# Causal grouped attention: the division by the row sums moved onto VectorE, straight from the PSUM bank

## The reference

```python
def _attention(x, Wq, bq, Wk, bk, Wv, bv, Wo, bo):   # x is layer-normed, (b, t, n) = (2, 512, 256)
    b, t, n = x.shape
    hd = n // Q_HEAD                                  # 16 query heads of 16, 4 key and value heads
    q, k, v = x @ Wq.T + bq, x @ Wk.T + bk, x @ Wv.T + bv
    ...                                               # split into heads; _rope on q and k
    k = jnp.repeat(k, rep, axis=1); v = jnp.repeat(v, rep, axis=1)
    att = jnp.einsum('bhqd,bhkd->bhqk', q, k) / scale
    att = jnp.where(causal[None, None], att, -jnp.inf)
    att = jax.nn.softmax(att, axis=-1)                # exponentials divided by their row sums
    y = jnp.einsum('bhqt,bhtd->bhqd', att, v)
    y = y.transpose(0, 2, 1, 3).reshape(b, t, n)
    return y @ Wo.T + bo
x = x + _L1_attn_a_ref(_layernorm(x), ...)
```

## Time and profile before

| | |
|---|---|
| median of 3 runs | 1567.59 us (1562.62 to 1567.86) |
| the profiled execution | 1567.11 us, of which the span is 1565.3 us |
| TensorE busy, whole span | 1439.8 us (92%), 10620 matmuls |
| VectorE busy | 965.8 us (62%) |
| ScalarE busy | 756.6 us (48%) |
| in the stage, 1126 to 1140 us: TensorE, VectorE, ScalarE busy | 12.68, 9.67, 7.50 of 14.00 us |
| granted clock there | 1.00 |

### The profile page before, as it was taken

How to read it: one execution, slowest core, us unless ns; L and a number is a source line. 1 busy time by engine, 2 the same in 40 slices (tenths; PEclk the granted TensorE clock), 3 DMA queues, 4 the chain that set the end, 5 groups by cost and what they waited for, 6 DMA issues and landing times. The chain is left out here.

```text
span 1565.3 us, 29243 instructions
## 1 busy us (share of the span) xinstructions
PE 1439.8 (92%) x10620; PEld 1117.4 (71%) x10646; DVE 965.8 (62%) x2214; ACT 756.6 (48%) x1877; POOL 561.7 (36%) x556
## 2 busy tenths in 40 slices
PE   6999999999899899899999999998898898988897
PEld 4778777787689767677777766895565596733586
DVE  5666667666575665656565557548655754565663
ACT  5565656656235334343443443452545362598352
POOL 2835629354136254515333101552000173100173
PEclk9999999999999999999999999999999999998998
DMA  4122231222272343303021007335000534121534
GB/s 147 55 90 68 84 101 46 86 63 90 82 313 85 122 130 112 120 6 114 24 74 69 1 1 287 142 120 192 1 1 2 197 102 147 31 60 33 187 99 138
DMA packets 57453, 149.48 MB, mean 95 GB/s; under 512 B 10224, under 2 KB 24688, under 8 KB 57200
## 3 DMA queue, kind: packets, MB, share of 16 engines
q1 hardware_dynamic: 39664, 89.58, 16.7%
q0 software_dynamic: 17664, 58.21, 11.0%
HBM read 104.77 MB, written 38.27 MB: 91 GB/s over the span
## 5 line engine op out<-in xcount | busy, mean ns | idle before, releaser
L145 POOL TENSOR_SCALAR ln_var<-ln_moments 128x4 f32<-128x4 f32 x16 | 4.1, 253 | 403.7 <-DVE ln_moments L130 251.3
L412 POOL DMA_INDIRECT expert_rows<-s_y,s_to_row x92 | 90.9, 989 | 57.9 <-ACT s_y L736 36.9
L1370 ACT ACTIVATE s_scratch<-s_bank,s_neg_max 128x128 f32<-128x128 f32 (+3 forms) x128 | 67.2, 527 | 88.0 <-DVE s_neg_max L1460 87.9
L1460 DVE TENSOR_REDUCE s_neg_max<-s_bank 128x1 f32<-128x128 f32 (+3 forms) x128 | 59.4, 486 | 55.2 <-PE s_bank L1260 55.0
L2797 POOL TENSOR_TENSOR s_w_hi<-s_w_raw,zero 128x1024 fp32r<-128x1024 f32 x25 | 55.6, 2223 | 100.1 <-PE s_memory L81 77.1
L1258 PE MATMUL s_bank<-s_k,s_q 128*128 128x128 f32 (+3 forms) x256 | 88.6, 442 | 1.5 <-DVE s_v L1455 0.8
L2464 ACT ACTIVATE s_exps<-s_bank,s_rms 128x512 f32<-128x512 f32 x128 | 77.9, 690 | 13.5 <-PE s_bank L2363 11.0
L953 DVE TENSOR_TENSOR s_h_e<-s_bank,s_silu_e 128x176 f32<-128x176 f32 x92 | 31.4, 341 | 83.5 <-ACT s_silu_e L724 79.6
L79 PE MATMUL s_bank<-xn_t_hi,s_w_hi 128*128 128x512 f32 x192 | 79.6, 415 | 1.7 <-DVE xn_t_lo L212 1.2
L405 POOL DMA_INDIRECT s_xg<-normed_rows,s_from_row x64 | 63.6, 994 | 38.5 <-DVE s_from_row L848 20.2
L1277 PE MATMUL s_bank<-s_probs_t,s_v 128*128 128x512 f32 (+3 forms) x256 | 74.7, 435 | 2.5 <-ACT s_probs_t L1378 2.5
(11 more groups left out here) (428 smaller groups left out, 4856.4 us busy)
## 6 DMA issues: line engine op xcount, KB each, us to landing
s_expert_w_lo<-experts_lo SPq DMA_DIRECT2D x32, 608.0 KB, 12.9
s_e_lo<-in_experts POOLq DMA_DIRECT2D x32, 304.0 KB, 3.1
experts_hi<-s_e_hi POOLq DMA_DIRECT2D x32, 304.0 KB, 2.5
experts_lo<-s_e_lo POOLq DMA_DIRECT2D x32, 304.0 KB, 2.9
s_expert_w_hi<-experts_hi SPq DMA_DIRECT2D x16, 608.0 KB, 12.1
s_w_raw<-in_wa_o SPq DMA_DIRECT2D x16, 512.0 KB, 3.5
s_yg<-expert_rows SPq DMA_DIRECT2D x32, 256.0 KB, 4.5
s_raw<-in_shared SPq DMA_DIRECT2D x16, 384.0 KB, 6.4
```

Of the source, the lines that this page charges most:

```text
L412: pool.indirect_dma_start(out=y_rows[:, :], out_offset=bass.IndirectOffsetOnAxis(ap=to_row[:, i:i + 1].bitcast(U32), axis=0), in_=y[:, i % ...
L1370: act.activation(probs[:, h % 2, r, 0:(r + 1) * P], score_bank(h, r), ACT.Exp, bias=neg_max[:, 4 * h + r:4 * h + r + 1], accum_out=row_sum ...
L1460: dve.tensor_reduce(neg_max[:, 4 * h + r:4 * h + r + 1], score_bank(h, r), AX.X, ALU.max, negate=True).then_inc(max_done, 1)
```

## The change

The attended bank is no longer copied or turned by TensorE. VectorE transposes it in blocks of 32 by 32 from PSUM to SBUF, takes the reciprocals of the sums (one column in 32), transposes them back, spread over their block, and multiplies the attended bank, still in PSUM, with them. The steps `turn` and `back` leave the ring, `att` is now read by the product (`o_scaled`), the high and low parts are taken from SBUF, and `scale_o(U - 1)` stands ahead of the first two maxima. Behind the last unit TensorE fills with 20 products on zeros where 5 and 6 stood around the turn back.

```diff
-        o_raw, inverse, o = sb("o_raw", [P, S]), sb("inverse", [P, TB, KV_HEADS]), sb("o", [P, S])
+        inverse, o = sb("inverse", [P, S]), sb("o", [P, S])
+        by_query, by_query_inverse = sb("by_query", [P, S]), sb("by_query_inverse", [P, S // SLOT])
...
                     if x == 1:
-                        order += [("turn", U - 1)] * (U > 0) + [("q", U + 2)] * (U + 2 < UNITS)
-                    if x == 3:
-                        order += [("back", U - 1)] * (U > 0)
+                        order += [("q", U + 2)] * (U + 2 < UNITS)
...
-            if kind in ("q", "shift", "att", "turn", "back"):
-                return {"q": q_rotated, "shift": q_shift_done, "att": o_copied, "turn": o_scaled, "back": o_lo_done}[kind], at[0] + 1
+            if kind in ("q", "shift", "att"):
+                return {"q": q_rotated, "shift": q_shift_done, "att": o_scaled}[kind], at[0] + 1
...
-            turn_o(UNITS - 1)
-            turn_o_back(UNITS - 1)
-            keep_busy(pe, res, held("back", UNITS - 1)[:, 1, :], 6)
+            keep_busy(pe, res, held("att", UNITS - 1)[:, 1, :], 20)
             project_out(len(OUTS) - 1)
...
             def high_o(U):
-                act.wait_ge(o_ready, U + 1)
+                act.wait_ge(o_scaled, U + 1)
...
-                act.activation(o_hi[:, U % 3, :], single("back", U), ACT.Copy).then_inc(o_hi_done, 1)
+                act.activation(o_hi[:, U % 3, :], o[:], ACT.Copy).then_inc(o_hi_done, 1)
...
             def scale_o(U):
-                by_head = single("turn", U).rearrange("p (t g s) -> p t g s", t=TB, s=SLOT)
-                dve.wait_ge(o_natural, U + 1)
-                dve.reciprocal(inverse[:], by_head[:, :, :, HD]).then_inc(inverse_done, 1)
...
+                dve.wait_ge(attended, TB * (U + 1))
+                attended_values = single("att", U)
...
+                dve.transpose(by_query[:], attended_values).then_inc(sums_turned, 1)
+                dve.wait_ge(sums_turned, U + 1)
...
+                dve.reciprocal(by_query_inverse[:], by_query[:].rearrange("p (b r) -> p b r", r=SLOT)[:, :, HD]).then_inc(sums_inverted, 1)
+                dve.wait_ge(sums_inverted, U + 1)
...
+                dve.transpose(inverse[:], by_query_inverse[:].unsqueeze(2).broadcast_to([P, S // SLOT, SLOT])).then_inc(inverse_done, 1)
                 dve.wait_ge(inverse_done, U + 1)
                 if U:
-                    dve.wait_ge(o_ready, U)
...
+                    dve.wait_ge(o_lo_done, U)
+                dve.tensor_tensor(o[:], inverse[:], attended_values, ALU.mult).then_inc(o_scaled, 1)
...
-                dve.tensor_tensor(o_lo[:, U % 3, :], single("back", U), f32(o_hi[:, U % 3, :]), ALU.subtract).then_inc(o_lo_done, 1)
+                dve.tensor_tensor(o_lo[:, U % 3, :], o[:], f32(o_hi[:, U % 3, :]), ALU.subtract).then_inc(o_lo_done, 1)
...
+                if U:
+                    scale_o(U - 1)
                 if ahead:
                     row_max(U + 1, 3, 0)
                     row_max(U + 1, 3, 1)
-                if U:
-                    scale_o(U - 1)
```

More of the change, by code:

```diff
@@ L1576, in causal_gqa_stage @@
         scores_ready, exp_done = sem("scores_ready"), sem("exp_done")
-        attended, o_copied, o_natural, inverse_done, o_scaled, o_ready, o_hi_done, o_lo_done = (
-            sem("attended"), sem("o_copied"), sem("o_natural"), sem("inverse_done"), sem("o_scaled"),
-            sem("o_ready"), sem("o_hi_done"), sem("o_lo_done"))
+        attended, sums_turned, sums_inverted, inverse_done, o_scaled, o_hi_done, o_lo_done = (
+            sem("attended"), sem("sums_turned"), sem("sums_inverted"), sem("inverse_done"),
+            sem("o_scaled"), sem("o_hi_done"), sem("o_lo_done"))
         out_ready, out_added = sem("out_ready"), sem("out_added")
@@ L1618, in ring_order @@
                     order += [("out", n) for n in outs_in(U)]
-            return order + [("turn", UNITS - 1), ("back", UNITS - 1), ("out", len(OUTS) - 1)]
+            return order + [("out", len(OUTS) - 1)]
         ring = ring_order()
@@ L1819, in attend @@
                 last.then_inc(attended, 1)
[L1821 to L1837, removed]
             def project_out(n):
@@ L1869, in _ @@
                         scores(U, j)
-                    if j == 0:
-                        if U:
[L1872 to L1876, removed]
+                    if j == 0 and U + 2 < UNITS:
+                        project_q(U + 2)
                     if j == 2 and not ahead:
@@ L1888, in _ @@
                         project_out(n)
-            turn_o(UNITS - 1)
-            turn_o_back(UNITS - 1)
-            keep_busy(pe, res, held("back", UNITS - 1)[:, 1, :], 6)
+            keep_busy(pe, res, held("att", UNITS - 1)[:, 1, :], 20)
             project_out(len(OUTS) - 1)
-            keep_busy(pe, res, held("back", UNITS - 1)[:, 1, :], 9)
+            keep_busy(pe, res, held("att", UNITS - 1)[:, 1, :], 9)
         @block.scalar
@@ L2033, in scale_o @@
             def scale_o(U):
[L2034 to L2036 removed]
+                dve.wait_ge(attended, TB * (U + 1))
+                attended_values = single("att", U)
+                if U:
+                    dve.wait_ge(sums_inverted, U)
+                dve.transpose(by_query[:], attended_values).then_inc(sums_turned, 1)
+                dve.wait_ge(sums_turned, U + 1)
+                if U:
+                    dve.wait_ge(inverse_done, U)
+                dve.reciprocal(by_query_inverse[:], by_query[:].rearrange("p (b r) -> p b r", r=SLOT)[:, :, HD]).then_inc(sums_inverted, 1)
+                dve.wait_ge(sums_inverted, U + 1)
+                if U:
+                    dve.wait_ge(o_scaled, U)
+                dve.transpose(inverse[:], by_query_inverse[:].unsqueeze(2).broadcast_to([P, S // SLOT, SLOT])).then_inc(inverse_done, 1)
                 dve.wait_ge(inverse_done, U + 1)
                 if U:
[L2039 to L2042 removed]
+                    dve.wait_ge(o_lo_done, U)
+                dve.tensor_tensor(o[:], inverse[:], attended_values, ALU.mult).then_inc(o_scaled, 1)
             def low_o(U):
                 dve.wait_ge(o_hi_done, U + 1)
[L2046 removed]
+                dve.tensor_tensor(o_lo[:, U % 3, :], o[:], f32(o_hi[:, U % 3, :]), ALU.subtract).then_inc(o_lo_done, 1)
             def add_to_stream(n):
```

12 lines of the change are left out of this document (removed).

## The result

The changed kernel takes 1589.68 us (median of 4 runs, 1587.18 to 1591.12), beside 1567.72 for the kernel before in the same set: a ratio of 1.0143, with a 95% interval of 1.012 to 1.0166. It is 22 us slower, where 17 were forecast. The profiled execution of after took 1591.12 us (span 1589.3), 24.0 more than that of before. The stage, from step 0 of unit 0 to the first product of the next stage, took 153.38 us (1098.09 to 1251.47) in place of 127.31 (1098.58 to 1225.89): 26.1 us more. The rest of the program, which the change does not touch, took 2.1 us less in this execution.

The account below looks back on a forecast made before the run. TensorE was taken to pace the unit, VectorE close behind, both meeting in the ring of four bank pairs. 2.4 + 6.0 + 5.5 + 0 + 3.5 = 17.4 us on 1567.11 gave 1584.5, range 1577 to 1591.

Parts of the forecast that it names:

- Bound and mechanism: TensorE paces the unit, VectorE close behind; TensorE waits for the division's product, which holds the attended bank pair.
- The four waits before step 1: Units 1, 2, 4 and 6, without output projection before: step 1 starts 2.60 after step 0 instead of 1.00.
- The chain, 2.48: VectorE's four division steps, first transpose to product, take 2.48 us, read from the same instructions in the next stage.
- The order terms: Delays from VectorE's order and the held pair: 2.4 (units 1, 2, 4, 6), 6.0 (units 3, 5), 5.5 (unit 7).
- The term of +0.3 in unit 6: Unit 6, which projects no query: attended product 10.15 after step 0 against 9.86, so +0.3 us.
- The tail and unit 7: Tail after unit 7 taken at nothing, between −0.5 and +0.5; inside unit 7 nothing of its +5.5 wait given back.
- The clock, 3.5: Falls of TensorE's clock behind the long waits cost 1.5 each in units 3 and 5, 0.5 in unit 7: 3.5 us.
- The clock holds: Rival: same mechanism, but TensorE's clock holds through the waits; 13.9 us, 1581; chance 0.12.
- The short waits cost the clock too: Rival: the four waits of about 1.5 us before step 1 add up to 1.7 each; 1591; chance 0.06.
- TensorE alone decides: Rival: pair free in time, seven units drop towards unit 0's 12.92; at most 9.9 us less, 1557.5; chance 0.05.
- Caught up: Rival: units after a wait run at unit 0's pace, leaving some 5 us lost; 1572; chance 0.07.
- The two rules cited: Trainium skill: idle stretches cost TensorE its clock (3.5 us rests on it); VectorE's transpose is quickest for 32 by 32 blocks.

Follow-up runs that it names:

- e9: Changed kernel with the division cut to one VectorE multiply by a constant, without transposes and reciprocal, nothing divided by the sums; 1575.65 us, ratio 1.0051.
- e2: Changed kernel with VectorE's division ahead of the addition to the stream, at the end of the same unit; 1575.95 us, ratio 1.0049.
- e5: Changed kernel with TensorE products of zeros in the long waits (15, 15, 22) and in the 1.43 us waits (six each); 1582.03 us, ratio 1.0078.
- e3: Changed kernel with TensorE products of zeros only in the long waits at the starts of units 3, 5 (15 each) and 7 (22); 1583.59 us, ratio 1.0096.
- e4: Changed kernel with six TensorE products of zeros before step 1 of units 1, 2, 4 and 6, long waits bare; 1592.07 us, ratio 1.0147.
- e10: Like e8, with the low part at the unit's end too and unit 7's output projections placed behind its first and third scores; 1558.51 us, ratio 0.9934.
- e8: Changed kernel with ScalarE copying the attended bank, division behind the unit's last maxima, everything behind it a unit later; 1566.39 us, ratio 0.9989.
- e11: e10 with two TensorE products of zeros (0.43 us) in each unit ahead of the shift; 1560.49 us, ratio 0.9956.
- e1: Changed kernel with ScalarE copying the attended bank to SBUF at the next unit's start, freeing the pair; VectorE divides from the copy; 1586.95 us, ratio 1.0104.

## Why the prediction was right, and where its sum was off

1. **Bound and mechanism: right.** TensorE waits for `s_o` at each place that was named. The four waits before step 1 were put at about 1.5 and are 1.43; the long ones 3.9, 3.9 and 5.5, measured 3.74, 3.74 and 5.31. e9 shows that they follow the chain, and e2 that the long ones come from the place behind the addition.
2. **The chain, 2.48: right**, 2.48 in the earlier trace rows and in after, with a PSUM bank as its input in both.
3. **The order terms: right in size.** +0.7 for units 1, 2 and 4 measured +0.59 (14.93 against 14.34); units 3 and 5, forecast 0.9 quicker once started, take 13.57 in place of 14.60 where the clock holds. The term of +0.3 in unit 6 was nothing: in e5, with its waits filled, its attended product follows 9.87 after step 0, exactly as before (1199.35 less 1189.48 is 9.87; the prediction has 9.86, a slip without weight). The tail and unit 7, taken at nothing, came to -0.7 (19.49 against 20.22). Together 12.1, forecast 13.9.
4. **The clock, 3.5: the step that failed.** In the profiled execution of after, the stage lies 153.38 - 139.4 = 14.0 above the sum of its units at full clock; over the runs, filling the waits gave back about 10. The prediction had three falls, one behind each long wait, each of about 3.4 us at the lower level, and priced them at 1.5, 1.5 and 0.5. One fall was sized well: 1.27 and 1.57 in the pairs of equal units above, 1.65 between units 3 and 5 of e3. Their number and length were wrong. The stage of after has 44 us at the lower level, in seven stretches: the three behind the long waits came as forecast, but last 3.4, 6.8 and 10.2, and four more (3.4 to 10.2) begin at waits of 0.85, 1.43, 0.97 and 1.43 in units 3, 4, 4 and 6. In unit 4 the second reaches the attended product, whose sixteen products take 3.21 in place of 1.71:

```profile
1177.37 3.21 PE L1816 MATMUL s_pair<-s_exps,s_v 128*32 128x512 f32 x16
```

   So the time lies inside the stated range in part by luck: the terms of the order were 1.8 too high, and that of the clock 6 to 10 too low.

5. **The rivals.** "The clock holds" (1581) is ruled out by the windows, though e5 comes within 1 us of its number. "The short waits cost the clock too" had 0.06 and came nearest in time, 1591 beside 1589.68. Its mechanism is only half of it: e2's unit 1 lost clock with no wait over 1.43, but e4, which fills just these waits, gained nothing in all. "TensorE alone decides" (1567.11 less 9.9 is 1557.2, where the prediction has 1557.5) was ruled out by the order that the change chose: e10 reaches unit 0's 12.92 with the same four VectorE steps. "Caught up" did not occur.
6. **The two rules cited.** By the Trainium skill ("TensorE: Matmul & The Clock Gate", section "Why this matters for your kernels") it is the long idle gap between bursts that costs the clock. The traces agree for the waits of 3.74 and 5.31: at each bare one, in after and in e4, the clock falls in the wait or within 1.3 us of its end. But low stretches also began in units where TensorE never waited over 1.43 (e2) or 0.85 (e8). The other rule, of the Trainium skill ("VectorE: DVE Perf Modes", section "Rules for kernel authors"), calls VectorE's transpose the quickest for blocks of 32 by 32. No run shows that: it takes 0.72, and four transposes held TensorE for 0.38. What e10 shows is that the move pays in a place where VectorE is idle.

What stays open: why a wait costs the clock in one unit and not in another. Units 1 and 2 of after have the same waits as unit 1 of e2, which lost its clock, and kept theirs. No run here separates that from what TensorE had done in the stretch before.

## What to carry to other kernels

An edit that takes work from the busiest engine gains only if the work lands where its new engine is idle: the same four instructions cost 12 us net ahead of the first maxima, before any fall of the clock, and behind the last ones they end with 0.58 us to spare. When a ring buffer's reader moves to a later engine, walk the ring to the step that wants that place next, and look for what stands ahead of the reader in its queue. And price the clock by units that will have waits, not by the longest waits alone: a single fall cost 1.3 to 1.7 us where equal units could be compared, and after had seven, some of them longer.

## What the runs showed that was not expected

- The clock fell behind short waits. In e8 the longest wait of unit 2 is 0.85 us and the unit's clock is 0.89; in e10 it is 0.41 and the clock 1.00. In the traces of all these kernels, each of the 53 low stretches of the stage begins during a wait of TensorE of 0.84 to 5.31 us or within 2 us of its end; units 1 to 6 of before, e10 and e11 have no wait over 0.50 and no low stretch. This is no threshold: equal waits without a fall stand beside them.
- Products of zeros in a wait can hold the clock: unit 4 of e3 is at 1.00 with 15 of them in the waits ahead of units 3 and 5, that of after at 0.78 without. They are no guarantee: unit 1 of e4, with six in its wait before step 1, is at 0.81, unit 1 of after at 1.00 without.
- VectorE's transpose of 128 by 512 in 32-bit values takes 0.70 to 0.72 from PSUM (after) and 0.70 or 0.71 from SBUF (e1, e10), so no difference is shown; the one that reads one value in each block spread over 32 columns takes 0.71, no less.
